# Attention's gate as a row scale in the copy of the outputs, the residual as an addition on GpSimd, the moments a quad later

## The reference, cut to what matters

```
x = x + tanh(g_xattn[0]) * L0_xattn(ctx, ctx, layernorm(x), ...)
x = x + tanh(g_ffn[0])   * L0_ffn(layernorm(x), ...)
x = x + tanh(g_xattn[1]) * L1_xattn(layernorm(x), ctx, ctx)
x = x + tanh(g_ffn[1])   * L1_ffn(layernorm(x), ...)
```

## Time and profile before

| | |
|---|---|
| Runs | 909.58, 906.32, 908.05 us; median 908.05 |
| Profiled execution | 910.07 us, of it 908.3 in the span of the trace |
| TensorE matmuls | 877.6 us busy, 97% of the span |
| VectorE | 600.4 us, 66% |
| ScalarE | 532.5 us, 59% |
| GpSimd | 133.2 us, 15% |
| Mean granted TensorE clock | 0.988 |
| Chain that ended last, by engine | PE 87%, DVE 5%, POOL 2%, DMA 2%, ACT 1%, issue 1% |

### The profile page before, as it was taken

How to read it: one execution, slowest core, us unless ns; L and a number is a source line. 1 busy time by engine, 2 the same in 40 slices (tenths; PEclk the granted TensorE clock), 3 DMA queues, 4 the chain that set the end, 5 groups by cost and what they waited for, 6 DMA issues and landing times.

```text
span 908.3 us, 13885 instructions
## 1 busy us (share of the span) xinstructions
PE 877.6 (97%) x4747; PEld 717.3 (79%) x4768; DVE 600.4 (66%) x1238; ACT 532.5 (59%) x916; POOL 133.2 (15%) x108
## 2 busy tenths in 40 slices
PE   6799999999999999989999989999999999999997
PEld 5799887777788888867777767878788888888886
DVE  5689764465654665579999865657755566666564
ACT  3225243344554344357777757777677867777774
POOL 5799300001012020012121310000000000000000
PEclk9799999999999999989999999999999999999999
DMA  8204150524532442013343234444444344444433
GB/s 293 86 1 135 36 157 18 158 73 160 168 123 82 144 143 59 24 30 114 111 125 102 82 116 125 139 136 140 140 140 143 95 140 139 139 149 151 147 122 105
DMA packets 70117, 106.47 MB, mean 117 GB/s; under 512 B 9216, under 2 KB 34176, under 8 KB 69664
## 3 DMA queue, kind: packets, MB, share of 16 engines
q1 hardware_dynamic: 69328, 105.44, 37.1%
q10 hardware_dynamic: 720, 0.14, 0.1%
HBM read 96.84 MB, written 8.72 MB: 116 GB/s over the span
## 4 chain that ended last, share of the span: by engine, by line
PE 87%; DVE 5%; POOL 2%; DMA 2%; ACT 1%; issue 1%; SPq 1%; DVEq 0%; ACTq 0%; POOLq 0%
PE bank L682 38%; PE bank L718 29%; PE bank L1525 3%; PE bank L1536 2%; PE bank L1516 2%; PE bank L1169 1%; PE bank L1168 1%; PE bank L1428 1%; PE bank L366 1%; PE bank L1166 1%; PE bank L1182 1%; DMA toeplitz<-in_kpad 1%; PE bank L1545 1%; PE bank L1510 1%; PE bank L347 1%
## 5 line engine op out<-in xcount | busy, mean ns | idle before, releaser
L479 ACT ACTIVATE y_hi<-y 128x512 fp32r<-128x512 f32 x200 | 124.0, 621 | 82.0 <-DVE y L562 81.4
L576 DVE TENSOR_TENSOR y<-y,gate_rows 128x512 f32<-128x512 f32 x124 | 85.8, 692 | 120.4 <-ACT y L468 117.6
L718 PE MATMUL bank<-y_hi,w_hi 128*128 128x512 f32 x400 | 157.3, 393 | 2.0 <-DVE y_lo L312 1.5
L718 PE MATMUL bank<-y_lo,w_hi 128*128 128x512 f32 x400 | 156.6, 391 | 0.0
L718 PE MATMUL bank<-y_hi,w_lo 128*128 128x512 f32 x400 | 155.9, 390 | 0.0
L312 DVE TENSOR_TENSOR y_lo<-y,y_hi 128x512 fp32r<-128x512 f32 x196 | 134.3, 686 | 30.0 <-ACT y_hi L479 29.6
L462 ACT ACTIVATE activated<-bank 128x512 f32<-128x512 f32 x136 | 81.1, 597 | 80.8 <-PE bank L682 76.2
L682 PE MATMUL bank<-x_hi_first,w_hi 128*128 128x512 f32 x264 | 106.2, 402 | 0.7 <-DVE w_lo L307 0.7
L682 PE MATMUL bank<-x_hi_first,w_lo 128*128 128x512 f32 x264 | 104.2, 395 | 0.0
L682 PE MATMUL bank<-x_lo_first,w_hi 128*128 128x512 f32 x264 | 104.1, 394 | 0.0
L682 PE MATMUL bank<-x_hi_last,w_hi 128*128 128x512 f32 x264 | 104.0, 394 | 0.0
(11 more groups left out here) (155 smaller groups left out, 1372.3 us busy)
## 6 DMA issues: line engine op xcount, KB each, us to landing
gate_rows<-gates SPq DMA_DIRECT2D x156, 256.0 KB, 3.7
w_raw<-in_wu SPq DMA_DIRECT2D x68, 256.0 KB, 2.6
w_raw<-in_wu SPq DMA_DIRECT2D x32, 384.0 KB, 4.2
k_blocks<-k_parts SPq DMA_DIRECT2D x128, 64.0 KB, 2.4
k_parts<-xn_split SPq DMA_DIRECT2D x32, 128.0 KB
v_slot<-in_v_rows SPq DMA_DIRECT2D x16, 256.0 KB, 2.7
ctx_windows<-in_ctx_win SPq DMA_DIRECT2D x3, 1024.0 KB, 10.8
toeplitz<-in_kpad SPq DMA_DIRECT2D x4, 512.0 KB, 9.4
```

The source lines that it names most:

```text
L479: act.activation(mem.yhi[:, K % S, :], mem.y[:, K % S, :], ACT.Copy).then_inc(s_yh, 1)
L576: dve.tensor_tensor(mem.y[:, K % S, :], mem.y[:, K % S, :], gate, ALU.mult).then_inc(s_yd, 1)
L718: last = pe.matmul(acc(s)[:, c, :], w_[:, Nu % S, wc], y_[:, K % S, :], start=(n == 0 and m == 0), stop=(n == U - 1 and m == 2), skip_grou ...
```

## The change

The gate tanh(g) moves from the residual into ScalarE's copy of the outputs: the outputs are still turned there (head rows on partitions), so the gate is a column of 128 values, tanh(g) for the 16 output rows of each group of 32 and 1.0 for the row of sums. VectorE builds that column once, at n == 2. The residual becomes a plain addition and is issued by GpSimd at t == 3, before `query_lo`; in `last_rows` it stays on VectorE. `scaled` waits for the residual of the block before, since `ov` is one buffer. The moments go from t == 0 to t == 1.

```diff
+            gate = sb("gate_column", [P, 1])
+            s_gf = sem("c_gate_column")
...
-                act.activation(oT[:].rearrange("p t q -> p (t q)"), o_bank, ACT.Copy).then_inc(s_oe, 1)
+                if b == 0:
+                    act.wait_ge(s_gf, 2)
+                act.activation(oT[:].rearrange("p t q -> p (t q)"), o_bank, ACT.Copy, scale=gate[:]).then_inc(s_oe, 1)
+
+            def gate_column(dve):
+                dve.memset(gate[:], 1.0).then_inc(s_gf, 1)
+                dve.wait_ge(s_gf, 1)
+                for g in range(4):
+                    last = dve.tensor_copy(gate[32 * g:32 * g + HD1, :], tg[32 * g:32 * g + HD1, 1:2])
+                last.then_inc(s_gf, 1)
...
             def scaled(dve, b):
                 dve.wait_ge(s_rc, b + 1)
+                if b > 0:
+                    dve.wait_ge(s_xd, b)
...
-            def residual(dve, b):
-                dve.wait_ge(s_sc, b + 1)
-                dve.scalar_tensor_tensor(X[:, b, :], ov[:], tg[:, 1:2], X[:, b, :], ALU.mult, ALU.add).then_inc(s_xd, 1)
+            def residual(eng, b):
+                eng.wait_ge(s_sc, b + 1)
+                eng.tensor_tensor(X[:, b, :], ov[:], X[:, b, :], ALU.add).then_inc(s_xd, 1)
...
             def c_gpsimd(pool):
                 for n in range(NQ):
                     b, t = n // 4, n % 4
+                    if t == 3 and b > 0:
+                        residual(pool, b - 1)
                     if t == 3 and b + 3 < NB:
                         query_lo(pool, b + 3)
...
-                    if t == 0 and b > 1:
+                    if t == 1 and b > 1:
                         moments(dve, b - 2)
...
                     if t == 3 and b > 0:
                         scaled(dve, b - 1)
-                        residual(dve, b - 1)
+                    if n == 2:
+                        gate_column(dve)
```

## The result

| | before | after |
|---|---|---|
| Median of 16 runs, us | 908.91 (906.09 to 910.80) | 910.61 (908.52 to 911.94) |
| Profiled execution, us | 910.07 | 911.42 |
| Span of the trace, us | 908.3 | 909.5 |
| VectorE busy, us | 600.4 | 597.7 |
| GpSimd busy, us | 133.2 | 143.3 |

The ratio of after to before is 1.0021, 95% interval 1.0011 to 1.0031: 1.9 us slower (1.0 to 2.8). That is under the 0.3% that the prediction set as "same", though the interval excludes no change. The forecast was 2.0 us slower.

A forecast was written before the change was run, and what follows sets the result against it. TensorE was taken to set the steady pace, 6.71 us a block. Column +0.8, n == 38 -0.46, router +0.2 and end +1.5 made +2.0 us, from a median of 908.05 to 910.0 us; range 906.6 to 912.2.

The forecast's parts named there:

- Steady blocks: Steady attention blocks: TensorE sets the 6.71 us pace, so the 0.5 us a block freed on VectorE is worth 0.
- Rival B: Steady blocks: VectorE is a co-limit, the 0.20 us at each third turn its wait; 2.6 us back, 907.4 us; chance 0.13.
- rival A: End of attention: GpSimd's added work there costs nothing, so +0.5 us in all, 908.6 us; chance 0.27.
- The block of n == 38: The 7.17 us block with eight moments aggregated: the late turn gets its data 0.7 us earlier, gaining 0.46 us.
- The scale in `out_copy`: ScalarE's copy of the outputs: a row scale costs 0, bound 0.1 us either way, ScalarE having room.
- The router at n == 44: The 7.01 us block: GpSimd still holds the router subtraction, the moments now stand behind it; about 0.2 us added.
- Smaller slips: At n == 30: small losses that the change might remove, at most 0.14 us, left out of the sum.
- The gate column: At n == 2: a memset and four tiny copies on VectorE delay subtractions TensorE waits for; 0.8 us added.
- The end: End of attention: GpSimd's later w_lo hold VectorE's routing operations, so the gates come late; 1.5 us added on TensorE.
- Rival C: Start of attention: the column lengthens TensorE's idle to 1.6 us, its clock falls; 3.3 us more, 913.3 us; chance 0.06.

The follow-up runs named there:

- e7a: The kernel before with the scaling done twice in blocks 1 to 11, 0.41 us more for VectorE a block; ratio to the kernel before 1.0048.
- e7b: The changed kernel with the scaling done twice in blocks 1 to 11; ratio to the kernel before 1.0025.
- e3: The changed kernel with only the router's low part moved from n == 44 to n == 46; ratio to the kernel before 1.0044.
- e2: The changed kernel with the gate column built earlier, in VectorE's idle time before the stage's first out_added; ratio to the kernel before 1.0006.
- e5: The kernel before with only the residual of block 14 moved to GpSimd, as a plain addition without the gate; ratio to the kernel before 1.0010.

## Why the prediction was right

The time was 1.9 us over the kernel before (2.0 forecast), and most terms came out as sized. Two things were left out of the sum: -0.16 at n == 30 and, by an estimate, +0.6 for the clock. So the agreement to 0.1 us is in part luck.

- *Steady blocks, 0.* Right, and by the reason given: 6.70 us a block, the label "issue", e7a and e7b. Rival B fell with that, and rival A with the wait before L727.
- *The block of n == 38, -0.46.* Measured -0.44.
- *The scale in `out_copy`, 0.* The copy lasts 0.09 us longer (0.69), and ScalarE had room for it, as said.
- *The router at n == 44, +0.2.* Measured +0.22, L321 held to the end of GpSimd's operation, the moments behind it; e3 takes it away. The 0.3 us by which the residual was to push `query_lo` back did not come (0.02 in this block).
- *Smaller slips, at most 0.14, left out.* The block with n == 30 gained 0.16. They should have been counted.
- *The gate column, +0.8.* Measured 0.80 to the first `out_rows`. The prediction gives the 128x8 operation once as 0.16 and reckons with the row's 0.17. The rule that the trace of before could not show, that an instruction is held when its partitions start in another quadrant than the last one's (Trainium skill, VectorE: DVE Perf Modes, section "Two Vector instructions with no wait between them"), is now borne out: 0.155 us a copy over four places, 0.08 on the same rows.
- *The end, +1.5.* Measured +1.34. One of the four operations got through between GpSimd's second and third w_lo, as forecast. The path behind was partly another. In the times of the trace before (0.68 us less, the shift of the first output product) the reciprocal started at 514.27, 0.75 us late and not 1.1. L905 was forecast to be held by y_lo(0), but it started ahead of it and ended at 516.8, not 518.2, so that the lateness was still only 0.7 us there. On the rest of the way 0.7 us more were lost: L908 took 0.81 instead of 0.22 and L915 1.29 instead of 0.43, each held by a y_lo, while L918 got back 0.8. That last one the forecast had overlooked. Of the 7.9 us from L908 to the gates before, it counted 0.9 as lost in L910, but 0.8 was lost in L918 too; before, with GpSimd's y_lo of that time, and after:
```profile
523.80 1.31 POOL L312 TENSOR_TENSOR y_lo<-y,y_hi 128x512 fp32r<-128x512 f32 x1 [2.40 <-ACT y_hi L479]
524.16 0.97 DVE L918 TENSOR_SCALAR sm<-sm 128x8 f32<-128x8 f32 x1
```
```profile
524.49 1.30 POOL L312 TENSOR_TENSOR y_lo<-y,y_hi 128x512 fp32r<-128x512 f32 x1 [2.47 <-ACT y_hi L479]
527.02 0.17 DVE L918 TENSOR_SCALAR sm<-sm 128x8 f32<-128x8 f32 x1
```
The gates were ready at 527.5, against 527.7 forecast. The mechanism (w_lo against the routing's first operations, then further meetings with y_lo) was right, but that its total came so near was luck, since its steps were off by up to 1.4 us and made up for each other.
- *Rival C, the clock.* Given 0.06 with the condition of an idle like that of 388 to 390. That condition was wrong: 1.58 us of idle among short pieces of work was followed by the fall in 4 of 7 traces. Its size was wrong the other way, 1.0 to 1.2 us instead of 3.3. Taken over the runs it would add 0.6 us to the sum if 4 of 7 is the true share, which seven traces don't settle but the recorded clocks bear out. It may be part of why e2 regained 1.6 us. The sum of the trace parts is +0.80 - 0.07 - 0.16 - 0.44 + 0.22 + 1.34 = +1.7 us without the clock and +2.3 with 0.6 for it; the measured 1.9 lies between.

The DMA waits that differ from trace to trace (the sixth block +0.30, the gate rows -0.75) are taken as not the change's: in the other traces the long block falls elsewhere or nowhere.

## What to carry to other kernels

Two engines that both look full need not both be the limit: look at a place where one had fallen behind and see whether the other's gap stays. Before work is moved to an engine whose operations can hold up another engine's, as GpSimd's and VectorE's do here, follow that engine's queue to the end of the loop, since a move that is free in the steady part can push the queue's tail into the next stage's critical operations; here putting one instruction behind another in that queue was enough. A one-time set-up of a few tiny instructions belongs in a gap of its engine, not in the ramp of a pipeline, where it is paid in full; here TensorE's clock fell on top of that in 4 of 7 traces. And where one trace is compared with another, look first whether the clock took the same course in both: here that alone was worth 1.1 us, as much as the effects looked for.

## What the runs showed of the hardware

- VectorE's operation with two SBUF inputs, issued while GpSimd reads SBUF, ends 0.1 to 0.3 us after GpSimd's operation (L321, L895, L896, L908, L915). With GpSimd's next one already waiting, one VectorE operation gets through (0.58 for L895) and the next waits a whole GpSimd operation (1.37 for L896). The same happened in e5. One operation with a single input was held as well: L918, a tensor_scalar of 128x8, took 0.97 us and ended with GpSimd's y_lo in each of the seven traces in which "gates" is 8.2, and 0.17 in the seven in which it is 9.5, where it meets none.
- An idle of 1.58 us, behind TensorE work in pieces with 0.3 to 1.6 us of idle between, was followed by a granted clock of 0.50 for some 3 us in 4 of 7 traces.
- A GpSimd addition of 128x256 takes 0.73 us, between 0.48 for 128 columns and 1.30 for 512.
- After the products of `values`, with 32 stationary columns, the next weight load starts at least 0.20 us late in every block of these traces, also where its data had long been there. The label on that gap can name an engine that isn't the cause.
